# High parts of the expert weights on POOL: a rounding copy with one input in place of a product with a column of ones

## The reference

```python
scores = sigmoid(x @ gate_w)                     # 32 experts
# the best 2 of 4 groups of experts, in them the best 6 experts of each row
weights = chosen scores / their sum
g = ragged_dot(xs, w_gate, group_sizes)          # xs: rows sorted by expert; 512 -> 352
u = ragged_dot(xs, w_up, group_sizes)            # 512 -> 352
d = ragged_dot(silu(g) * u, w_down, group_sizes) # 352 -> 512
expert_out = sum over the 6 choices of d * weights
shared = (silu(x @ sw_gate) * (x @ sw_up)) @ sw_down   # 512 -> 704 -> 512
return expert_out + shared
```

## Time and profile before

| | us |
|---|---|
| median of three runs | 2290.17 (2286.09 to 2292.93) |
| profiled execution, span from first to last instruction | 2293.4 |
| PE busy | 1971.3 (86%) |
| DVE busy | 1182.9 (52%) |
| POOL busy | 1116.9 (49%) |
| ACT busy | 565.1 (25%) |

### The profile page before, as it was taken

How to read it: one execution, slowest core, us unless ns; L and a number is a source line. 1 busy time by engine, 2 the same in 40 slices (tenths; PEclk the granted TensorE clock), 3 DMA queues, 4 the chain that set the end, 5 groups by cost and what they waited for, 6 DMA issues and landing times. The chain is left out here.

```text
span 2293.4 us, 33594 instructions
## 1 busy us (share of the span) xinstructions
PE 1971.3 (86%) x10564; PEld 1441.9 (63%) x10565; DVE 1182.9 (52%) x2230; ACT 565.1 (25%) x1164; POOL 1116.9 (49%) x552
## 2 busy tenths in 40 slices
PE   5956887968896689998799999999999999997991
PEld 3423443743343233333599989999999999996880
DVE  2554443557776767774774335444444455443330
ACT  3320222401114345443222212121212121211110
POOL 0000000003457356564044558666666788777886
PEclk9977998888996789999899999999999999998995
DMA  3043101402225366711135445545445555654999
GB/s 116 0 112 105 46 27 44 158 32 85 83 71 186 133 213 211 230 52 43 40 105 182 170 142 165 168 151 170 154 150 167 183 163 178 193 165 118 209 202 211
DMA packets 199487, 305.98 MB, mean 133 GB/s; under 512 B 16472, under 2 KB 94808, under 8 KB 199416
## 3 DMA queue, kind: packets, MB, share of 16 engines
q1 hardware_dynamic: 141624, 187.24, 26.0%
q0 software_dynamic: 21504, 50.93, 9.6%
q10 hardware_dynamic: 36288, 66.84, 8.2%
HBM read 186.42 MB, written 118.55 MB: 133 GB/s over the span
## 5 line engine op out<-in xcount | busy, mean ns | idle before, releaser
L2456 PE MATMUL psum<-e_gu_high,e_rowT_high 128*128 (+1 forms) x1272 | 430.5, 341 | 22.3 <-POOL e_gu_low L2111 14.0
L2456 PE MATMUL psum<-e_gu_low,e_rowT_high 128*128 (+1 forms) x1272 | 410.3, 324 | 0.0
L2180 ACT ACTIVATE e_silu<-psum 128x352 f32<-128x352 f32 x159 | 73.9, 465 | 873.2 <-PE psum L2461 847.1
L2456 PEld LDWEIGHTS psum<-e_gu_high,e_rowT_high 128*128 128x128 f32 x1272 | 241.8, 190 | 50.2 <-issue 46.2
L2461 PE MATMUL psum<-e_gu_high,e_rowT_low 128*128 (+1 forms) x1272 | 256.8, 324 | 0.0
L2456 PEld LDWEIGHTS psum<-e_gu_low,e_rowT_high 128*128 128x128 f32 x1272 | 242.8, 191 | 3.5
L2258 DVE TENSOR_TENSOR e_midT_low<-psum,e_midT_high 128x256 fp32r<-128x256 f32 x159 | 67.5, 424 | 341.1 <-ACT e_midT_high L2189 326.1
L2461 PEld LDWEIGHTS psum<-e_gu_high,e_rowT_low 128*128 128x128 f32 x1272 | 214.5, 190 | 0.0
L2476 PE MATMUL psum<-e_d_high,e_midT_high 128*128 (+3 forms) x477 | 188.0, 394 | 1.0 <-ACT e_midT_high L2189 1.0
L2476 PE MATMUL psum<-e_d_low,e_midT_high 128*128 (+3 forms) x477 | 188.5, 395 | 0.0
L2107 POOL TENSOR_TENSOR e_gu_high<-f_gu_in,e_ones 128x1408 fp32r<-128x1408 f32 x31 | 78.6, 2534 | 198.1 <-PE psum L2461 181.8
(11 more groups left out here) (380 smaller groups left out, 3950.6 us busy)
## 6 DMA issues: line engine op xcount, KB each, us to landing
d_sorted<-f_hs SPq DMA_DIRECT2D x32, 1048.0 KB, 10.4
e_row<-d_sorted ACTq DMA_DIRECT2D x125, 262.0 KB
d_y<-f_arena ACTq DMA_DIRECT2D x127, 256.0 KB
f_gu_in<-in_L_ffn_w_gate SPq DMA_DIRECT2D x32, 704.0 KB, 5.2
f_gu_in<-in_L_ffn_w_up SPq DMA_DIRECT2D x32, 704.0 KB, 5.1
f_d_in<-in_L_ffn_w_down SPq DMA_DIRECT2D x32, 512.0 KB
d_y<-f_hs SPq DMA_DIRECT2D x8, 1024.0 KB, 5.8
f_d_in<-in_L_ffn_w_down SPq DMA_DIRECT2D x32, 192.0 KB
```

Of the source, the lines that this page charges most:

```text
L2456: nc.tensor.matmul(bank[:, 0:M].unsqueeze(1), rowT_high[par][:, k, :], w[:, bass.ds(buffer, 1), k, at:at + M], start=(k == 0 and n == 0), ...
```

## The change

Four products on POOL in `split` and `split_down` lose their second input, the first column of the tile `ones` spread over all columns, and become copies into the same F32R tiles. What is subtracted afterwards, the semaphores and the waits stay.

```diff
-                nc.gpsimd.tensor_tensor(d_high[:, par, 0:2, :], d_in[:, 0:2, :], ones[:, 0:1].unsqueeze(2).broadcast_to((P, 2, D)), ALU.mult)
-                nc.gpsimd.tensor_tensor(d_high[0:LAST_M, par, 2, :], d_in[0:LAST_M, 2, :], ones[0:LAST_M, 0:1].broadcast_to((LAST_M, D)), ALU.mult).then_inc(high_ready, 1)
+                nc.gpsimd.tensor_copy(d_high[:, par, 0:2, :], d_in[:, 0:2, :])
+                nc.gpsimd.tensor_copy(d_high[0:LAST_M, par, 2, :], d_in[0:LAST_M, 2, :]).then_inc(high_ready, 1)
...
-                nc.gpsimd.tensor_tensor(gu_high[:, par, :, 0:M], gu_in[:, :, 0:M], ones[:, 0:1].unsqueeze(2).broadcast_to((P, CC, M)), ALU.mult).then_inc(high_ready, 1)
+                nc.gpsimd.tensor_copy(gu_high[:, par, :, 0:M], gu_in[:, :, 0:M]).then_inc(high_ready, 1)
...
-                nc.gpsimd.tensor_tensor(gu_high[:, par, :, M:2 * M], gu_in[:, :, M:2 * M], ones[:, 0:1].unsqueeze(2).broadcast_to((P, CC, M)), ALU.mult).then_inc(high_ready, 1)
+                nc.gpsimd.tensor_copy(gu_high[:, par, :, M:2 * M], gu_in[:, :, M:2 * M]).then_inc(high_ready, 1)
```

## The result

| | before | after |
|---|---|---|
| median of the runs, us | 2289.80 (2286.09 to 2292.93, 4 runs) | 2274.38 (2266.79 to 2278.27, 4 runs) |
| profiled execution: span, us | 2293.4 | 2275.9 |

The ratio is 0.9929, with a 95% interval of 0.9906 to 0.9952: 16.3 us less (11.0 to 21.5). Forecast were 10.8 us less and 2279.4 us. The direction is right, but the time lies 0.6 us under the low end of the range.

A forecast was written before the change was run, and what follows sets the result against it. PE was taken to bound the kernel until 2031 us, then POOL with its DMAs. Three late splits at 3.59 us save 10.8 us: 2290.17 - 10.8 = 2279.4 us, range 2275 to 2309.

The forecast's parts named there:

- The price of a copy: In POOL's splits: a copy costs 0.833 ns a column plus 198 ns fixed, saving 3.59 us a split.
- The rivals with two and three steps: POOL's copies cost about two steps a column (no gain, 2290; 0.21 with prices between) or three (slower, 2307.7; 0.26).
- The end's term: After 2031 us, POOL's splits of sets 31 to 33 each save 3.59 us, 10.8 us in all.
- The rival in which the landings eat most of it: In the run of 87 gathers, landing waits grow by the gain, leaving less than half: some 2286; chance 0.05.
- The failed step: From 1345 to 2031 us PE bounds, so split length changes nothing there while POOL keeps up; gain zero.
- the mark itself: Start of the end stretch: the first gather stays near 2031 us; if it moves, the prediction is wrong.
- PE's two waits: PE's waits for the gate parts of sets 32 and 33 shrink from 6.87 and 7.12 to 1.0 and 3.5 us.
- POOL's waits for PE: Before 2031 us, shorter splits make POOL wait longer for PE to leave buffers: about 97 us more.

The follow-up runs named there:

- e1: Kernel before with copies only in the splits of sets 30 to 33, products in the other 27: 2280.27 us, ratio 0.9955.
- e3: Kernel after, but in sets 3 to 29 each copy is made twice, first into the low part's tile: 2271.61 us, ratio 0.9931.
- e7: Kernel after, with splits of sets 3 to 29 padded by a second, shorter copy so SP's issues fall as before: 2276.19 us, ratio 0.9958.
- e9: Kernel after, unchanged, measured once more: 2276.08 us, ratio 0.9940.
- e4: Kernel before with its products; PE reads one expert number at a tile's border, not two: 2285.98 us, ratio 0.9987.
- e5: Kernel before with its products; SP's issues of the up and down transfers moved later: 2278.05 us, ratio 0.9958.
- e8: Kernel after without the waits for the third gather's landing before the splits of sets 31 to 33: 2260.51 us, ratio 0.9882.
- e10: Kernel after without the three landing waits before late splits, and with one border read of PE, not two: 2259.56 us, ratio 0.9865.
- e2: Kernel before with copies in the splits of sets 3 to 29, products in the last four: 2283.63 us, ratio 0.9983.

## Why the prediction was right and where it failed

- *The price of a copy* was right to 1 to 2.5%: (1360 - 1036) / (1408 - 1024) = 0.844 ns a column and 172 ns fixed, against 0.833 and 198. The rivals with two and three steps fell with it. The Trainium skill (GPSIMD Engine Reference, Engine selection) calls one-input work roughly line rate, and the trace agrees, at 0.844 ns a column; the 1.8 cycles an element of that page's section on elementwise cost, 1.5 ns as an estimate, did not hold for a copy.
- *The end's term*, 10.8 us, was right: the splits gave 10.9, the landings took 1.1 back, and the end got 10.1 shorter (9.95 to 10.95 in after, e1, e3, e7 and e9). The rival in which the landings eat most of it fell.
- *The failed step* is this sentence: "A faster or slower split does nothing for the end there, as long as POOL keeps up." With it the range held no gain for the stretch before 2031 us, and its low end was the end's gain with scatter alone. The split's length also places SP's transfers, which I had down as "move along with it" at no price. In before they came just ahead of PE's border reads; the late loads that this made are what the loop got back, 6.3 us in after. The prediction named the mark itself: the first gather was to stay near 2031, and it moved to 2023.51 (1.4 us of that came before the first split).
- *Why misled.* PE busy for 99.7% of the stretch reads like a full engine. The profile models the ends of matmuls, and its share is the same for after's loop, with tiles of 6.70 us, and for before's, with some of up to 6.95. The idle time of the weight loads and the count of matmuls told them apart, and I had looked at neither.
- *PE's two waits* were to be 1.0 and 3.5 us and are 3.23 and 3.38 in after's timeline of PE. The second fits; the first is 2.2 us longer than the sum. The loop's gain is not the reason, since it moved the first gather, and so POOL, by as much. Counted from the first gather, PE came to this wait after 39.03 us and before after 40.68, 1.65 us sooner, where the sum had it come no sooner; and POOL's part was ready 5.29 us sooner and not 5.9, as the two landings ahead of it took 0.8 us longer:

```profile
2065.77 0.56 PE L2456 MATMUL psum<-e_gu_high,e_rowT_high 128*128 x1 [3.23 <-POOL e_gu_low L2111]
...
2092.23 0.43 PE L2456 MATMUL psum<-e_gu_high,e_rowT_high 128*128 x1 [3.38 <-POOL e_gu_low L2111]
```

- *POOL's waits for PE* grew by 86.9 us to 268.7 (28 times), where 97 were forecast; the loop that got 6.3 us shorter is most of that difference.

## What to carry to other kernels

A faster step beside a full engine can still move the end, because it shifts the transfers that it releases: ask how long before the other engines' small reads they will be issued, and keep such reads away from borders or single. A busy share near one doesn't say that an engine runs at its pace; compare the period of its tiles and the idle time of its weight loads that is put down to issue. Where a wait for a landing stands between two pieces of the bounding engine's work, try whether the second piece has any need of it: here that took 15.4 us off the end, where the change took 10.1.

## What the runs showed of the hardware

- A register load from SBUF by PE's sequencer takes 0.30 us in the median, but 0.7 to 1.1 us in before where it starts 0.8 to 1.3 us behind the issue of an up or a down transfer (all 28 reads over 0.8 us stand there). Full DMA engines alone do not do it: 2.1 us behind an issue a read took 0.298 us with q1 at 105.0%. Nor does it hang on POOL's work: the reads were as slow with copies (e7) as with products. In e3 the reads over 0.8 us started 0.24 to 0.92 us behind the issue, so the cause stays open.
- PE's loop of two tiles has two paces, 6.70 us for every tile or 6.70 and 6.78 in turn, which last for all of a loop (after, e4, e5, e8, e10) or change within it (e2, e3, e9). Its cause stays open.
- A copy that rounds to fp32r costs what a memset costs by the column (0.844 ns, memset 0.833).
